# A new order of two lanes' turns on every engine of a kernel of eight graph and feed-forward layers

## The reference

```
x = x + G0(layernorm(x), adj)   # three rounds: m = adj @ (h @ w_k), h = GRU(m, h)
x = x + F0(layernorm(x))        # router over 8 experts, top 2, gelu FFN of width 256
x = x + G1(layernorm(x), adj)   # graph attention, leaky relu, masked softmax, elu
x = x + F1(layernorm(x))        # slice attention: 8 heads, 64 slices
x = x + G2(layernorm(x), adj)   # mean of the neighbours' messages
x = x + F2(layernorm(x))        # Mamba2 block: projection, conv, silu, chunked state sum
x = x + G3(layernorm(x), adj)   # two layers of masked softmax attention with 4 heads
x = x + F3(layernorm(x))        # mixture of depths: gelu FFN on the upper half of the nodes
```

## Time and profile before

| | us |
|---|---|
| median of 3 runs | 3326.07 |
| lowest and highest run | 3326.05, 3329.3 |
| span of the profiled execution | 3325.0 |
| busy in it: PE, DVE, ACT, POOL | 3186.7, 2205.0, 1787.2, 630.2 |
| fillers of the full halves (L1066) | 4350 matmuls, 310.1 busy |
| ACT table loads | 204, 261.7 busy |
| one full half | 198.8 |

### The profile page before, as it was taken

How to read it: one execution, slowest core, us unless ns; L and a number is a source line. 1 busy time by engine, 2 the same in 40 slices (tenths; PEclk the granted TensorE clock), 3 DMA queues, 4 the chain that set the end, 5 groups by cost and what they waited for, 6 DMA issues and landing times.

```text
span 3325.0 us, 63136 instructions
## 1 busy us (share of the span) xinstructions
PE 3186.7 (96%) x24992; PEld 2271.8 (68%) x24992; DVE 2205.0 (66%) x6966; ACT 1787.2 (54%) x3341; POOL 630.2 (19%) x788
## 2 busy tenths in 40 slices
PE   8899999999999999999999999999999999999999
PEld 5766667666676666667666676666667666666687
DVE  3566667676676766667666676676767676676654
ACT  2346465474646647465574646546465564646534
POOL 0002212031121302212031121302112130121302
PEclk9989999999999999999999999999999999999999
DMA  3000000000000000000000000000000000000000
GB/s 136 1 6 3 17 7 1 23 1 20 5 17 7 1 23 1 17 8 5 19 2 20 4 17 7 1 23 1 20 4 17 7 1 20 1 4 4 1 8 5
DMA packets 28775, 40.72 MB, mean 12 GB/s; under 512 B 1344, under 2 KB 17728, under 8 KB 28224
## 3 DMA queue, kind: packets, MB, share of 16 engines
q1 hardware_dynamic: 28480, 36.67, 3.5%
HBM read 28.28 MB, written 4.19 MB: 10 GB/s over the span
## 4 chain that ended last, share of the span: by engine, by line
PE 72%; DVE 14%; ACT 9%; issue 3%; POOL 1%; DVEq 0%
PE ps L445 59%; ACT scratch L1074 6%; PE ps L909 6%; DVE scratch L1393 4%; DVE scratch L1387 3%; PE ps L454 2%; DVE scratch L1879 2%; DVE scratch L1896 1%; PE ps L1062 1%; POOL scratch L2105 1%; DVE scratch L1390 1%; ACT adjf L1074 1%; PE ps L617 1%; ACT xT L1074 1%; ACT L1074 1%
## 5 line engine op out<-in xcount | busy, mean ns | idle before, releaser
L1074 ACT ACTIVATE scratch<-scratch 128x512 f32<-128x512 f32 (+4 forms) x832 | 567.6, 694 | 139.1 <-DVE scratch L1879 69.1
L445 PE MATMUL ps<-xT,weights_sb 128*128 128x512 f32 x1152 | 565.8, 601 | 7.3 <-ACT xT L1074 7.2
L445 PE MATMUL ps<-scratch 128*128 128x128 f32 (+6 forms) x4608 | 529.1, 379 | 27.1 <-ACT adjf L1074 6.6
L2105 POOL TENSOR_SCALAR scratch<-scratch 128x512 f32<-128x512 f32 x512 | 347.4, 696 | 975.0 <-DVE scratch L1886 975.0
L445 PE MATMUL ps<-weights_sb,scratch 128*128 128x128 f32 (+3 forms) x3840 | 489.3, 277 | 1.4
L445 PEld LDWEIGHTS ps<-weights_sb,scratch 128*128 128x128 f32 (+3 forms) x3840 | 438.3, 182 | 51.4 <-issue 39.3
L445 PEld LDWEIGHTS ps<-scratch 128*128 128x128 f32 (+5 forms) x4608 | 340.6, 160 | 127.0 <-issue 62.6
L1074 ACT ACTIVATE scratch<-ps 128x512 f32<-128x512 f32 (+2 forms) x384 | 212.1, 561 | 330.3 <-PE ps L445 213.7
L2088 POOL TENSOR_TENSOR rstd<-ve,minus_half 128x4 f32<-128x4 f32 x126 | 128.8, 1022 | 1232.1 <-DVE ve L1390 1230.5
L1879 DVE CUSTOM_DVE_ANT_0 scratch<-ps,nomask 128x512 f32<-128x512 f32 x512 | 334.3, 684 | 41.5 <-PE ps L445 40.4
L909 PE MATMUL ps<-weights_sb,scratch 128*128 128x128 f32 x2048 | 308.3, 278 | 29.9 <-ACT adjf L1074 7.8
(11 more groups left out here) (167 smaller groups left out, 4547.8 us busy)
## 6 DMA issues: line engine op xcount, KB each, us to landing
adj<-adj SPq DMA_DIRECT2D x16, 1024.0 KB, 5.8
weights_sb<-weights SPq DMA_DIRECT2D x1, 4605.0 KB, 18.9
x_in<-x SPq DMA_DIRECT2D x16, 256.0 KB, 2.8
scratch<-scratch SPq DMA_DIRECT2D x32, 128.0 KB, 2.3
out<-x SPq DMA_DIRECT2D x16, 256.0 KB, 2.5
scratch<-raw SPq DMA_DIRECT2D x1, 1645.0 KB, 22.3
weights_sb<-weights SPq DMA_DIRECT2D x1, 499.0 KB, 6.0
scratch<-raw SPq DMA_DIRECT2D x1, 384.0 KB, 5.0
```

The lines of the kernel that those rows point to most:

```text
L445: return pe.matmul(o, lhsT, rhs, start=start, stop=stop, **k)
L1074: return act.activation(o, a, func, **k)
L2105: pool.tensor_scalar(p, p, cut(g, G3_RI + n, 1), 1.0, ALU.mult, ALU.mult).then_inc(s["att_p"], 1)
```

## The change

Only the five strings of the full halves are written anew. Each holds the same number of `e` and `l` as before (PE 126 and 128, ACT 64 and 86, DVE 97 and 131, POOL 10 and 41, SP 3 and 3), so that no step is added or left out, and each lane keeps its own order. The digits in `PE_TURNS` fall from 145 to 65, so the fillers of a full half from 290 to 130. Before they stood in 27 groups all over the half; now there are four: 40 before the columns of F0 and 12 behind them, and 48 and 30 around the second turn of G3's layer 1, beside G1. The strings of the first and the last half are untouched. The new file is two lines shorter, so L1066 is L1064 there, and so on.

```diff
 SP_TURNS = (
-    "ellele"
+    "elleel"
 )
...
 PE_TURNS = (
-    "ee7777eeeeelelleleleelllllleeeeeellll7777llllell7777777777777777777777777777777leellllllllleleeeeel"
...
+    "eeeeeleeellleleeellllleleeeeeeelelllellllelleeeeeleeeellllllllell22222222222222222222eeee777777llllelllleeeeelllleeee"
...
 ACT_TURNS = (
-    "eleeeleleeellllllllelllllleellllllelleeeeeleeeleeeleelllleeeellllleeleelllllleelllllllllleeeeeeeleee"
...
+    "leeeeleleeeeleelllllllelellllleeelllllllleeeeeeeleeeelleellllllllleeleelllllleellllllllleleeeeeeeeeeeleellllellllllell"
...
 POOL_TURNS = (
-    "lllellellllllllllllllllllellllllllllelellllleeeelle"
+    "llllelellllllllllllllllelellllelellelllleeelllllllle"
 )
```

More of the change, by code:

```diff
@@ L102 @@
 PE_TURNS = (
[L103 to L106, removed]
+    "eeeeeleeellleleeellllleleeeeeeelelllellllelleeeeeleeeellllllllell22222222222222222222eeee777777llllelllleeeeeelllleeee"
+    "eeeeeelllleelllleeleeeeelleelelleeleeeleeeleeellleeelllleleleeleellllllleeeelleeelleleleeleeeell2222222222222222222222"
+    "22l333333333333333llleeeelelellleellellleleelelllllellllelllleeellllellellelllleeee"
 )
 ACT_TURNS = (
-    "eleeeleleeellllllllelllllleellllllelleeeeeleeeleeeleelllleeeellllleeleelllllleelllllllllleeeeeeeleee"
-    "eeellellllllllllllellllellllleleleeleeelellelleeee"
+    "leeeeleleeeeleelllllllelellllleeelllllllleeeeeeeleeeelleellllllllleeleelllllleellllllllleleeeeeeeeeeeleellllellllllell"
+    "lleleeleeellellllllleleeleeellll"
 )
 DVE_TURNS = (
-    "leelllleeeleeelllllllllellllllllllellellllleeellllellleleleeleleeeeelleleleeleeeeelelelelllelllllell"
-    "lelellllllellllleelllelllleleeleeeeeeeeellllllllllllelllellllellleleeellelllleelleleeeleleeeeeeeeell"
-    "lllleeeleelleleeleeleeelelee"
+    "leelllleeeeeellllllllleleeeeelllllllllllelllleelleeeleeeelelllllleleeeeeeeelleeelllllelllelllllellllllllelllllellllele"
+    "llelllleleleeleeeeeeeellllllleleleelelelelllelllleleeleeeleleeeeleeeleellllllllleeeellellleleeelllellleeelelee"
 )
 POOL_TURNS = (
-    "lllellellllllllllllllllllellllllllllelellllleeeelle"
+    "llllelellllllllllllllllllelllellelllelleeelllllllle"
 )
```

## The result

The changed kernel takes 3314.92 us (median of 5, 3313.13 to 3316.05) against 3326.59 us before (5 runs): a ratio of 0.9964 with a 95% interval of 0.9951 to 0.9976, 11.7 us faster. The forecast was 3269, 57 us faster, with a range from 3200 to 3334: the sign was right and the size not, a fifth of what was forecast.

A forecast was written before the change was run, and what follows sets the result against it. PE, busy 96% of the span, was taken as the bound. Stretches of 50.6 + 63.8 + 29.0 + 51.6 = 195.0 us against 198.8 save 3.8 per half, 15 x 3.8 = 57, giving 3269 us; range 3200 to 3334.

The forecast's parts named there:

- D: Full half's stretch from the F1 column transposes to the next half: 44.2 us before, forecast 51.6, with no fillers.
- third rival: PE clock falls to half speed in D once per half, at most 5.1 us each: 3346 us, chance 0.14.
- the signs put on record: Stretches near 51, 64, 29, 52 us; clock 0.50 in D means third rival; wrong if B and D grow over 19.
- B: Full half's stretch from the F0 to the G1 column transposes: 56.2 us before, forecast 63.8, receiving F2's tail.
- the condition I set for it: In D, one wait as long as the first half's, some 2 us, brings one clock fall per half.
- A: Full half's stretch from the G0 to the F0 column transposes: 65.5 us before, forecast 50.6.
- from 26.7 to about 14: G0's second round in A shortens to about 14 us with the three gate products together; the surest step.
- C: Full half's stretch from the G1 to the F1 column transposes: 32.9 us before, forecast 29.0, with 4.8 of waiting.
- worth nothing by themselves: Across the full half, fillers hide waits; 160 fewer pay only where useful matmuls take their place.
- first rival: Fillers were on PE's path: each of 160 per half is saved, 9.0 us per half, 3192 us, chance 0.13.
- Second rival: B and D together wait 3.8 us more than forecast on the next engine: about 3326 us, chance 0.13.

The follow-up runs named there:

- the kernel with 28 fillers: Changed kernel plus two groups of 14 fillers in D, ahead of the ratio product and of f1_attend: 3259.33 us, ratio 0.9794.
- The splices: Strings joined at G1's columns: new A and B with old C and D, 3240.08 us (3238.37 without D's fillers); old A and B with new C and D, 3412.82.

## Why the prediction was wrong in size

- **The clock.** "The clock falls in D" was the third rival, with 0.14. It is what happened, in every full half, and the signs put on record read it so: 0.50 in D, B at 63.8, and B and D together longer by 18.4 and 20.0 us in turn, where 19 was the limit. The fall took 55.6 us of the gain, by the kernel with 28 fillers. The step that failed is the condition I set for it: one wait of about 2 us with PE empty, taken from the first half. Two waits of 0.8 us, 3 us apart, among small products were enough, so the sum had a term for the clock in D of nothing where 3.7 us per half were due. I had written that "the longest idle time I can place is about 1 us", which was right and no protection. The price of that rival was bounded by half of 10.3 us, 5.1 per half; it is 2.9 and 4.5, some 3.7 in the mean. Its time of 3346 was too high for that reason and by the 10 us below.
- **A**, "from 26.7 to about 14": the rounds take 14.9, 14.6 and 17.0 us, and 5.1 to the columns, where 14.9, 14.2, 16.6 and 4.9 were forecast. Right, and 1.0 us too short in all. Here the first row is the start of A, the L468 rows are the second and the third round, and L505 is g0_back, as in the earlier trace rows:

```profile
1969.64 0.60 PE L452 MATMUL ps<-weights_sb,x_in_ln 128*128 128x128 f32 x4
...
1984.58 0.66 PE L468 MATMUL ps<-weights_sb,xT 128*128 128x128 f32 x4
...
1999.13 0.66 PE L468 MATMUL ps<-weights_sb,xT 128*128 128x128 f32 x4 [0.17 <-DVE xT L1391]
...
2016.14 0.66 PE L505 MATMUL ps<-weights_sb,xT 128*128 128x128 f32 x4
...
2021.22 1.10 PE L452 MATMUL ps<-weights_sb,xn 128*128 128x128 f32 x4 [1.03 <-DVE xn L1388]
```

- **B**: forecast 63.8, measured 63.8. The exact hit is partly luck, since its 6.1 us of waiting was an estimate; that VectorE, busy for 45.7 of 63.8 us, is no bound fits it.
- **C**: forecast 29.0, measured 26.8. The waiting taken there was 4.8 us and is 2.6 by the same sum, where it was 3.7 before: C's waiting fell with the work that left, where I had it grow. No run shows which waits these are.
- **D** without the fall: forecast 51.6, measured 52.06.
- **Fillers**: "worth nothing by themselves" was nearly right, against the first rival: 0.6 of the 2.5 us in B was on the path, by the kernel before without any. But I gave them one job, to fill a wait, and they had a second, to keep the clock up. The same kernel has three falls per half.
- **Second rival** (the next engine takes the gain): not what happened, as B is at its forecast.

With the clock held, the sum would have been 10 us too high: 15 x (1.0 + 0.0 - 2.2 + 0.5) = -11 us, and 3269 - 11 = 3258, against 3259.33 measured. The sum of the four stretches was sound, though its errors of 1.0, -2.2 and 0.5 us in part cancel, which is luck; the one term that was a yes or no was put down as no. The splices add that the whole gain lay in A and B, and that the new C and D lost 19 us of it even without a fall.

The Trainium skill's rule that activity lifts the half clock ("TensorE: Matmul & The Clock Gate", "Part 1: The HAM clock gate") spoke against this change. These runs agree that what PE did shortly before decides, and show that fillers as such don't: two kernels without any in D kept the clock, and one with 28 of them in the wrong place did not, in 12 of 15 halves.

## What to carry to other kernels

When an order takes work away from a place where PE waits, look at PE's busy share in short windows there, not at the longest single wait, and run one variant with a few cheap matmuls in the waits: if it gets faster, the clock had fallen. A reordering of a long loop is better costed and tested by stretches between fixed points, since a splice at such a point told here that one part of the change gave 87 us and the other took 75 back, 56 of them by the clock. On an engine that serves two lanes strictly in order, a step put ahead of one that is ready can cost more than its own time.

## What the runs showed of the hardware that I had not expected

- The clock fell 0 to 2.5 us after 4 us in which PE was busy for 62% and no wait was over 0.78 us (windows of the changed kernel), and a group of 14 bf16 matmuls of 0.8 us was enough to prevent it.
- In the full halves the low times come in the same few lengths, 3.4, 6.8 and 10.2 us, once 13.7, though PE had work again at once, and one and the same code gets one or the other from half to half, though A, B and C ahead of it are alike to 0.06 us.
- Where a kernel stands at that edge, its runs scatter: 3302 to 3342 us in 10 runs of one program, with a mean granted clock of 0.979 to 0.967, against 6.4 us in 10 runs of the kernel before without D's fillers.
